# Layer 0 of a two-layer recurrent network: how the router weights reach the expert rows

## The chip, the cores and the metric

One Trainium2 chip, one of its cores. The core has five engines that run side by side: TensorE (PE), VectorE (DVE), ScalarE (ACT), GpSimd (POOL) and SyncE (SP, which here only issues DMAs), and 16 DMA engines. The metric is device time of one launch in microseconds.

## The reference, cut to what matters

The input is 16 sequences of 256 tokens, 128 channels, fp32. Two layers follow one another. Layer 0 computes `x + s * g`, where `s` is a recurrence over the tokens and `g` is the silu of a mixture of experts on the same normalised tokens:

```python
# s: for every token n, per head (8 heads, state 16 x 16)
S = exp(g)[..., None] * S + a_t[..., None] * bS[:, :, None, :] + k_t[..., None] * v_t[:, :, None, :]
# router: sigmoid scores, 4 of 8 groups, 8 of 64 experts, weights normalised, times 2.5
w_dense = jnp.zeros((T, E)).at[jnp.arange(T)[:, None], tidx].add(tw)
# experts: all 64 on all tokens, each result scaled by its router weight (0 for most)
hmid = jax.nn.silu(x @ wg) * (x @ wu)
acc + cw[:, None] * (hmid @ wdn)
```

Layer 1 (attention and a second expert block) is not touched here.

## The kernel before, in words

Layer 0 works in 8 tiles (`NT`) of 32 time steps of all 16 sequences: 512 tokens (`TOK`) a tile. In each tile two things run side by side.

- **The recurrence, on DVE.** `tile` runs 32 steps of nine instructions each (L666 to L680). Between the steps it does work for the next tile: after steps 3, 6, 7 and 12 the four stages of its layer norm (L525 to L541), after step 20 its `route` (L546 to L600), which ends with the router weights `cw`. After the last step come `finish`, `prepare_norm`, `finish_norm` and `prepare` (L612 to L651).
- **The experts, on PE, ACT and POOL.** Two experts of 64 hidden rows make a pair that fills 128 rows; there are 32 pairs and one shared expert. Before the change a pair takes three PSUM slots (`SLOTS = 3 * PAIRS + 2`), used in a ring of four: gate (three matmuls), up (three matmuls), and a third one, L486, in which a selector matrix `sel` of zeros and ones is multiplied with `cwt`, the router weights transposed. This product copies the weights of the pair's two experts to its 64 rows each, as a 128x512 tile in PSUM. ACT evicts the three slots (L380) into `act_g`, `act_u` and `act_c`, each a ring of three pairs. POOL multiplies gate by up (L302) and that by `act_c` (L306) into `hid`. PE then multiplies with the down weights, two pairs later (`LAG`, L457), into one accumulating bank.

What sets the order: each engine's program is written out, and semaphores tie them. ACT may overwrite a ring place of pair p only when `hid` of pair p - 3 is ready. In ACT's list of slots three pieces of work for the next tile are put in: `norm` at slot 24 (pair 8), `project` at pair 15, and `recurrence_inputs` at slot 66 (pair 22). After the last pair ACT copies the sum (L382), applies the silu (L384, the gate), then waits for DVE's sum of squares (L695) with L387. Only then do L357 and L362 follow; L362 copies the transposed weights `cwt` of the next tile out of PSUM, and PE starts the next tile's pairs behind it. DVE in turn waits for L387 before it can go on into its next tile. So the two sides meet once per tile at this point, and in the middle at the norm and at the projection.

SP issues every DMA: at the start inputs and weights, and in each tile the projected `z` through DRAM (L241, L244), the next tokens (L204), the gate (L248) and the result `y` (L252).

Semaphores named below: `moe_slot_filled` is PE's count of PSUM slots, `moe_slot_copied` ACT's count of evictions, `moe_hidden_ready` POOL's count of `hid`.

Of the kernel before, what the change touches and what calls it, by code (L numbers as in the profile page):

```python
# [7 lines left out]
F32 = mybir.dt.float32  # L8
F32R = mybir.dt.float32r
BF16 = mybir.dt.bfloat16  # L10
ALU = mybir.AluOpType
# [3 lines left out]
P = 128  # L15
# [3 lines left out]
TOK = B * TP  # L19
# [18 lines left out]
NEG = -1e30  # L38
SLOTS = 3 * PAIRS + 2
STEPS = 9  # L40
# [20 lines left out]
def layer0(nc, d, scratch, sem):  # L61

    z_dram, y_dram, g_dram = scratch
    with ExitStack() as ctx:
# [4 lines left out]
        ident = sb("ident", [P, P])  # L69
        onehot = sb("onehot", [P, E0])  # L70
        tri = sb("tri", [P, G0 * G0])
# [12 lines left out]
        wd = sb("wd", [P, PAIRS + 1, D])  # L84
        sel = sb("sel", [P, E0, F0], F32R)
        x_sb = sb("x_sb", [P, NS, D])
# [16 lines left out]
        cw_sum = sb("cw_sum", [P, NS])  # L103
        cws = sb("cws", [P, NS, 2 * E0], F32R)
        cwt = sb("cwt", [P, TOK], F32R)
        RING = 3
        act_g = sb("act_g", [P, RING, TOK])
        act_u = sb("act_u", [P, RING, TOK])
        act_c = sb("act_c", [P, RING, TOK])
        hid1 = sb("hid1", [P, TOK])  # L110
# [21 lines left out]
        s_eps = sem("eps_set")  # L132
        s_sel = sem("selectors_ready")
        s_w1t_ps = sem("transposed_small_in_psum")
# [21 lines left out]
        s_rt = sem("router_chain")  # L156
        s_cws = sem("router_weights_split")
        s_cwt_ps = sem("router_weightsT_in_psum")
        s_cwt = sem("router_weightsT_ready")
        s_slot = sem("moe_slot_filled")  # L160
        s_ev = sem("moe_slot_copied")
# [20 lines left out]

        LN, PREP, POST, ROUTE = 3, 20, 5, 57


        LN_AT, ROUTE_AT = (3, 6, 7, 12), 20
        PROJECT_PAIR, NORM_SLOT, INPUT_SLOT = 15, 24, 66
        SMALL = 13

# [8 lines left out]
        def _(sp):  # L198
# [8 lines left out]
            sp.dma_start(ident[:, :], d["c_ident"]).then_inc(s_small, 16)  # L207
            sp.dma_start(onehot[:, :], d["c_onehot"]).then_inc(s_small, 16)
            sp.dma_start(tri[:, :], d["c_tri"].rearrange("(o c) -> o c", o=1).to_broadcast([P, G0 * G0])).then_inc(s_small, 16)
# [69 lines left out]
        @block.gpsimd  # L279
        def _(pool):  # L280
            pool.memset(eps[:, 0:1], LN_EPS).then_inc(s_eps, 1)
            pool.memset(eps[:, 1:2], RNN_EPS).then_inc(s_eps, 1)

            for k, (w, c) in enumerate(chunks):
                pool.wait_ge(s_stage[k % 3], 16 * (k // 3 + 1) if w < 2 else 16 * (k // 3 + 2))
                parts = ([((wg_hi, wg_lo), (wu_hi, wu_lo))[w] + (c * CH * F0, CH * F0, 0)] if w < 2 else
                         [(wg_hi, wg_lo, E0 * F0, F0, 0), (wu_hi, wu_lo, E0 * F0, F0, F0)])
                for m, (hi, lo, at, n, off) in enumerate(parts):
                    src = stages[k % 3][:, off:off + n]
                    pool.tensor_scalar(hi[:, at:at + n], src, 1.0, 1.0, ALU.mult, ALU.mult).then_inc(s_hi_tmp, 1)  # L290
                    pool.wait_ge(s_hi_tmp, k + 1 + m)
                    pool.tensor_tensor(lo[:, at:at + n], src, hi[:, at:at + n].bitcast(F32), ALU.subtract).then_inc(s_split, 1)

            with pool.Fori(0, NT) as t:
                for p in range(PAIRS + 1):

                    pool.wait_ge(s_ev, t * SLOTS + min(3 * p + 3, SLOTS))
                    g, u, c = act_g[:, p % RING, :], act_u[:, p % RING, :], act_c[:, p % RING, :]
                    if p < PAIRS:
                        if p > 0:  # L300
                            pool.wait_ge(s_h, t * (PAIRS + 1) + p)
                        pool.tensor_tensor(hid1[:, :], g, u, ALU.mult).then_inc(s_h1, 1)  # L302
                        pool.wait_ge(s_h1, t * PAIRS + (p + 1))
                        if p >= 2:
                            pool.wait_ge(s_dn, t * (PAIRS + 1) + (p - 1))
                        pool.tensor_tensor(hid[:, p % 2, :], hid1[:, :], c, ALU.mult).then_inc(s_h, 1)  # L306
                    else:
                        pool.wait_ge(s_dn, t * (PAIRS + 1) + (p - 1))
                        pool.tensor_tensor(hid[0:F0, p % 2, :], g[0:F0], u[0:F0], ALU.mult).then_inc(s_h, 1)

        @block.scalar
        def _(act):
# [46 lines left out]
            def tile(t, par, ahead):  # L359

                act.wait_ge(s_cwt_ps, t + 1)
                act.activation(cwt[:, :], pb[:, 1, :], ACT.Copy).then_inc(s_cwt, 1)  # L362

                act.wait_ge(s_gst, t * 16)
                act.wait_ge(s_split, len(chunks) + 1)
                for r in range(SLOTS):
                    p, what = r // 3, r % 3
# [3 lines left out]
                    if ahead and r == 3 * PROJECT_PAIR:  # L371
                        project(t + 1, 1 - par)
                    if ahead and r == INPUT_SLOT:
                        recurrence_inputs(t + 1, 1 - par)
                    act.wait_ge(s_slot, t * SLOTS + (r + 1))
                    if what == 0 and p >= RING:

                        act.wait_ge(s_h, t * (PAIRS + 1) + (p - RING + 1))
                    dst = (act_g, act_u, act_c)[what][0:n, p % RING, :]
                    act.activation(dst, pb[0:n, r % 4, :], ACT.Silu if what == 0 else ACT.Copy).then_inc(s_ev, 1)  # L380
                act.wait_ge(s_dn, (t + 1) * (PAIRS + 1))
                act.activation(yt, pb[:, 4, :], ACT.Copy).then_inc(s_y, 1)  # L382
                act.wait_ge(s_g_ps, t + 1)
# [18 lines left out]
        def _(pe):  # L402
# [38 lines left out]
            def experts(t, par, ahead):  # L441
                pe.wait_ge(s_cws, t + 1)
                pe.wait_ge(s_ev, t * SLOTS)
# [3 lines left out]
                for s in range(NS):  # L447
                    last = pe.transpose(pb[:, 1, P * s:P * (s + 1)], cws[:, s, :].bitcast(F32), ident[:, :])
                last.then_inc(s_cwt_ps, 1)
                pe.wait_ge(s_cwt, t + 1)  # L450
                pe.wait_ge(s_sel, 1)
                pe.wait_ge(s_wd, 32)
# [13 lines left out]
                for p in range(PAIRS + 1):  # L466
                    if ahead and p == PROJECT_PAIR:
                        pe.wait_ge(s_ev, t * SLOTS + 3 * p)
                        project(t + 1, 1 - par)
                        pe.wait_ge(s_zc, (t + 2) * NS)  # L470
                        pe.wait_ge(s_sc, t + 2)
                    pe.wait_ge(s_split, 2 * (2 * p // CH + 1))
                    for what, (w_hi, w_lo) in enumerate(((wg_hi, wg_lo), (wu_hi, wu_lo))):
                        r = 3 * p + what
                        slot_free(r)
# [29 lines left out]
        def _(dve):  # L505
# [37 lines left out]
            def route(t):  # L543
# [1074 lines left out]
def constants():  # L1618
# [3 lines left out]
        "c_ident": np.eye(P, dtype=f),  # L1622
        "c_onehot": np.tile(np.eye(E0, dtype=f), (2, 1)),
        "c_tri": np.tril(np.ones((G0, G0), f), -1).reshape(-1),
# [48 lines left out]
```

## Time and profile before

| | us |
|---|---|
| median of 3 runs | 2451.81 |
| range of the runs | 2451.44 to 2452.27 |
| the profiled execution, its time | 2448.52 |
| the profiled execution, its span | 2446.7 |

The span is what the hardware profiler saw between the first and the last instruction; 1.8 us lie around it. A row of a profile is one execution. On the page, busy time is summed over instructions of an engine, and the 40 digits show in which part of the span it lies: one digit is 61.2 us. Layer 0 fills about the first 22 and a half digits and layer 1 the rest.

### The profile page before, as it was taken

The page shows a single profiled execution, that of the slowest core. Times are in us where ns is not written, and L with a number is a line of the kernel's source. Part 1 is how long each engine was busy: PE and PEld are TensorE (multiplying, and loading weights), DVE is VectorE, ACT ScalarE, POOL GpSimd, SP SyncE. Part 2 cuts the span into 40 slices and gives each one's busy share as a digit, 9 for nine tenths or more (in the row PEclk, how much of TensorE's full clock was granted, in tenths as well). Part 3 has the DMA queues.
Part 4 walks back from the last instruction along what each step waited for, and adds up shares of the span by engine and source line. Part 5 has one row for each costly group of instructions (what it writes and reads, how often), then busy time and mean ns, then how long its engine had stood idle before and what let it go on. Part 6 is the DMA issues. An engine that isn't in the chain of part 4 may idle for free. (4 is left out here: it accounts for less than half of the span.)

```text
span 2446.7 us, 35810 instructions
## 1 busy us (share of the span) xinstructions
PE 1809.3 (74%) x10242; PEld 1356.9 (55%) x10242; DVE 1758.5 (72%) x4377; ACT 1062.2 (43%) x1765; POOL 758.0 (31%) x577
## 2 busy tenths in 40 slices
PE   1585584664845855847586089898999999999998
PEld 1353352442523533425353078888888877777776
DVE  4999999999999999999999554444444434444443
ACT  2463362453634633625453045444555344444443
POOL 2764473463635644735586000000000000000000
PEclk8797797787878877977798589999999899999999
DMA  6220020200200201202000321010110100000000
GB/s 113 51 49 9 8 42 10 34 19 5 49 10 1 49 9 16 38 5 44 5 5 5 90 44 23 18 21 15 20 22 10 48 8 14 13 13 13 13 13 11
DMA packets 140823, 60.08 MB, mean 25 GB/s; under 512 B 94599, under 2 KB 135036, under 8 KB 140668
## 3 DMA queue, kind: packets, MB, share of 16 engines
q1 hardware_dynamic: 140668, 58.24, 11.8%
q8 instruction: 70, 1.15, 0.2%
q14 instruction: 85, 0.70, 0.1%
HBM read 37.10 MB, written 21.10 MB: 24 GB/s over the span
## 5 line engine op out<-in xcount | busy, mean ns | idle before, releaser
L302 POOL TENSOR_TENSOR hid<-act_g,act_u 128x512 f32<-128x512 f32 x256 | 341.1, 1332 | 530.4 <-ACT act_c L380 512.7
L405 PE MATMUL pb<-xt_hi,wg_hi 128*128 128x512 f32 (+1 forms) x264 | 211.1, 800 | 208.7 <-ACT cwt L362 168.7
L306 POOL TENSOR_TENSOR hid<-hid,act_c 128x512 f32<-128x512 f32 x256 | 344.4, 1345 | 20.1
L457 PE MATMUL pb<-hid,wd 128*128 128x512 f32 x528 | 301.9, 655 | 35.2 <-POOL hid L306 33.9
L1515 DVE SCALAR_TENSOR_TENSOR l_acc<-l_pb,l_gtok,l_acc 128x128 f32<-128x128 f32 x512 | 144.3, 344 | 253.3 <-PE l_pb L1168 253.3
L1168 PE MATMUL l_pb<-l_xt,l_big 128*128 128x512 f32 (+1 forms) x1024 | 296.3, 411 | 35.0 <-DVE l_rope L1447 25.1
L1557 DVE TENSOR_REDUCE l_mrow<-l_pb 128x2 f32<-128x256 f32 (+1 forms) x256 | 137.2, 555 | 171.4 <-PE l_pb L1168 168.4
L380 ACT ACTIVATE act_g<-pb 128x512 f32<-128x512 f32 (+1 forms) x264 | 158.3, 600 | 220.9 <-PE pb L407 215.5
L1168 PEld LDWEIGHTS l_pb<-l_big,l_hid 128*128 128x128 f32 x2048 | 247.1, 192 | 10.5
L1096 ACT ACTIVATE l_hid<-l_pb,l_cols 128x512 f32<-128x512 f32 x256 | 169.4, 688 | 183.0 <-PE l_pb L1168 182.7
L1168 PE MATMUL l_pb<-l_big,l_hid 128*128 128x128 f32 x2048 | 247.9, 275 | 0.0
L1168 PEld LDWEIGHTS l_pb<-l_xt,l_big 128*128 128x128 f32 x1024 | 192.7, 198 | 72.7 <-DVE l_rope L1447 23.7
L405 PE MATMUL pb<-xt_hi,wu_hi 128*128 128x512 f32 (+1 forms) x264 | 112.5, 426 | 154.9 <-ACT act_g L380 154.9
L405 PEld LDWEIGHTS pb<-xt_hi,wg_hi 128*128 128x128 f32 (+1 forms) x264 | 53.5, 203 | 271.9 <-ACT cwt L362 171.2
L666 DVE TENSOR_TENSOR products<-zr,rs 128x512 f32<-128x512 f32 x256 | 175.4, 685 | 14.1 <-issue 6.1
L1133 ACT ACTIVATE l_big<-l_pb 128x768 f32<-128x768 f32 x128 | 104.6, 817 | 176.0 <-PE l_pb L1327 89.5
L669 DVE TENSOR_REDUCE rs<-products 128x32 f32<-128x512 f32 x256 | 175.7, 686 | 0.0
L667 DVE TENSOR_TENSOR products<-zr,rs 128x512 f32<-128x512 f32 x256 | 174.1, 680 | 0.0
L380 ACT ACTIVATE act_u<-pb 128x512 f32<-128x512 f32 (+1 forms) x264 | 157.7, 598 | 20.0 <-PE pb L407 10.5
L457 PEld LDWEIGHTS pb<-hid,wd 128*128 128x128 f32 x528 | 89.2, 195 | 125.1 <-POOL hid L306 107.0
L380 ACT ACTIVATE act_c<-pb 128x512 f32<-128x512 f32 x256 | 152.2, 594 | 0.0
L405 PEld LDWEIGHTS pb<-xt_hi,wu_hi 128*128 128x128 f32 (+1 forms) x264 | 53.4, 202 | 174.3 <-ACT act_g L380 161.0
(300 smaller groups left out, 4105.4 us busy)
## 6 DMA issues: line engine op xcount, KB each, us to landing
z_scratch<-zs SPq DMA_DIRECT2D x128, 81.0 KB, 4.2
zr<-z_scratch SPq DMA_DIRECT2D x8, 1296.0 KB, 8.4
x_sb<-in_L_attn_x_dram SPq DMA_DIRECT2D x32, 64.0 KB, 3.1
g_scratch<-act_u SPq DMA_DIRECT2D x8, 256.0 KB, 2.3
y_scratch<-yo SPq DMA_DIRECT2D x8, 256.0 KB, 2.0
l_xs<-in_L_attn_x_dram SPq DMA_DIRECT2D x32, 64.0 KB, 1.9
l_ys<-y_scratch SPq DMA_DIRECT2D x128, 16.0 KB, 1.7
l_gs<-g_scratch SPq DMA_DIRECT2D x8, 256.0 KB, 3.0
```

The lines of the kernel that those rows point to most:

```text
L302: pool.tensor_tensor(hid1[:, :], g, u, ALU.mult).then_inc(s_h1, 1)
L306: pool.tensor_tensor(hid[:, p % 2, :], hid1[:, :], c, ALU.mult).then_inc(s_h, 1)
L380: act.activation(dst, pb[0:n, r % 4, :], ACT.Silu if what == 0 else ACT.Copy).then_inc(s_ev, 1)
L405: pe.matmul(out, l_hi, r_hi, start=first, stop=False, skip_group_check=True)
L457: last = pe.matmul(pb[:, 4, :], wd[0:n, p, :], hid[0:n, p % 2, :], start=(p == 0), stop=(p == PAIRS), skip_group_check=True)
L666: dve.tensor_tensor(products[:, 2:4], two(ZG), twice, ALU.mult).then_inc(s_st, 1)
L667: dve.tensor_tensor(products[:, 0:2], two(ZF), twice, ALU.mult).then_inc(s_st, 1)
L669: dve.tensor_reduce(rs[:, 3, 0:2], products[:, 2:4], AX.X, ALU.add).then_inc(s_st, 1)
L1096: act.activation(hid[:, r % HR, :], pb[:, 2 + r % 3, :], ACT.Relu, bias=cols[:, r:r + 1]).then_inc(s_hid, 1)
L1168: return pe.matmul(out, l, r, start=start, stop=stop, skip_group_check=True)
L1515: dve.scalar_tensor_tensor(out=acc[:, s, :], in0=pb[:, 5 + e % 2, sub], scalar=gtok[par][:, s, e:e + 1], in1=acc[:, s, :], op0=ALU.mult, o ...
L1557: dve.tensor_reduce(mrow[:, k, 2 * j:2 * j + 2], src, AX.X, ALU.max).then_inc(s_ua_dve, 1)
```

## The change

The third slot of a pair is dropped. `cwt` is kept as 64 rows of 512 tokens, one row per expert, in plain fp32. For each pair a DMA issued from ACT's own queue reads the pair's two rows, each 64 times, and writes a 128x512 tile (256 KB) into `act_c`, which is now a ring of five places (`CRING`) with a semaphore for each. The first two loads of a tile are issued right behind the copy of `cwt`, and load p + 2 stands ahead of ACT's gate eviction of pair p. POOL waits for the pair's load ahead of its second product. PE no longer multiplies by `sel`, ACT no longer evicts it, DVE no longer makes `sel` nor the split `cws`, and SP no longer loads `onehot`. The transpose of the weights becomes a product with the identity.

```diff
-SLOTS = 3 * PAIRS + 2
+SLOTS = 2 * PAIRS + 2
-        cwt = sb("cwt", [P, TOK], F32R)
-        RING = 3
+        cwt = sb("cwt", [E0, TOK])
+        RING, CRING = 3, 5
-        act_c = sb("act_c", [P, RING, TOK])
+        act_c = sb("act_c", [P, CRING, TOK])
...
-        PROJECT_PAIR, NORM_SLOT, INPUT_SLOT = 15, 24, 66
+        PROJECT_PAIR, NORM_SLOT, INPUT_SLOT = 15, 16, 44
-            sp.dma_start(onehot[:, :], d["c_onehot"]).then_inc(s_small, 16)
...
                         pool.wait_ge(s_h1, t * PAIRS + (p + 1))
+                        pool.wait_ge(*spread(t, p))
...
-                act.activation(cwt[:, :], pb[:, 1, :], ACT.Copy).then_inc(s_cwt, 1)
+                act.activation(cwt[:, :], pb[0:E0, 1, :], ACT.Copy).then_inc(s_cwt, 1)
+
+                def load_weights(p):
+                    src = cwt[2 * p:2 * p + 2, :].unsqueeze(1).to_broadcast([2, F0, TOK])
+                    act.dma_start(act_c[:, p % CRING, :], src).then_inc(s_c[p % CRING], 16)
...
+                act.wait_ge(s_cwt, t + 1)
+                load_weights(0)
+                load_weights(1)
...
+                    if what == 0 and p + 2 < PAIRS:
+                        load_weights(p + 2)
-                    dst = (act_g, act_u, act_c)[what][0:n, p % RING, :]
+                    dst = (act_g, act_u)[what][0:n, p % RING, :]
...
-                    last = pe.transpose(pb[:, 1, P * s:P * (s + 1)], cws[:, s, :].bitcast(F32), ident[:, :])
+                    last = pe.matmul(pb[0:E0, 1, P * s:P * (s + 1)], cw[:, s, :], ident[:, :], start=(s == 0), stop=True, skip_group_check=True)
...
-                    if p < PAIRS:
-                        r = 3 * p + 2
-                        slot_free(r)
-                        pe.matmul(pb[:, r % 4, :], sel[:, 2 * p:2 * p + 2, :].rearrange("p a b -> p (a b)"), cwt[:, :], start=True, stop=True).then_inc(s_slot, 1)
...
-            dve.tensor_copy(sel[:, :, :], over(onehot[:, :], F0)).then_inc(s_sel, 1)
...
-                dve.tensor_tensor(cw[:, :, :], cw[:, :, :], over(cw_sum[:, :], E0), ALU.mult).then_inc(s_rt, 1)
-                dve.wait_ge(s_rt, c.next())
-                dve.tensor_copy(cws[:, :, 0:E0], cw[:, :, :]).then_inc(s_rt, 1)
-                dve.wait_ge(s_rt, c.next())
-                dve.tensor_tensor(cws[:, :, E0:2 * E0], cw[:, :, :], cws[:, :, 0:E0].bitcast(F32), ALU.subtract).then_inc(s_cws, 1)
+                dve.tensor_tensor(cw[:, :, :], cw[:, :, :], over(cw_sum[:, :], E0), ALU.mult).then_inc(s_cw, 1)
```

The start of a tile on ACT, before the change (from the copy of `cwt` to the first eviction of pair 1):

```order
L362 ACTIVATE cwt<-pb 128x512 [waits router_weightsT_in_psum]
L364 REGISTER_ALU
L375 ISA [waits expert_weights_split,gate_stored]
L380 ACT_TABLE_LOAD
L380 ACTIVATE act_g<-pb 128x512 [waits moe_slot_filled]
L375 REGISTER_ALU
L380 ACTIVATE act_u<-pb 128x512 [waits moe_slot_filled]
L375 REGISTER_ALU
L380 ACTIVATE act_c<-pb 128x512 [waits moe_slot_filled]
L375 REGISTER_ALU
L380 ACTIVATE act_g<-pb 128x512 [waits moe_slot_filled]
```

and after it (`expert_weights_split` is the count of the expert weights that POOL splits at the start of the program; `router_weightsT_ready` tells that `cwt` is written):

```order
L364 ACTIVATE cwt<-pb 64x512 [waits router_weightsT_in_psum]
L370 REGISTER_ALU
L368 DMA act_c<-cwt 128x1x512 [waits router_weightsT_ready,expert_weights_split,gate_stored]
L368 DMA act_c<-cwt 128x1x512
L384 ISA
L368 DMA act_c<-cwt 128x1x512 [waits moe_slot_filled]
L391 ACT_TABLE_LOAD
L391 ACTIVATE act_g<-pb 128x512
L384 REGISTER_ALU
L391 ACTIVATE act_u<-pb 128x512 [waits moe_slot_filled]
L384 REGISTER_ALU
L368 DMA act_c<-cwt 128x1x512 [waits moe_slot_filled]
```

The eviction of `act_c` has gone, and a DMA issue stands ahead of every gate eviction, behind that eviction's own wait.

POOL's products of pair 2 before the change (L302 multiplies gate by up, L306 by the weights):

```order
L302 TENSOR_TENSOR hid<-act_g,act_u 128x512 [waits moe_hidden_ready]
L303 REGISTER_ALU
L306 TENSOR_TENSOR hid<-hid,act_c 128x512 [waits moe_hidden_used,moe_product_ready]
L297 REGISTER_ALU
L301 REGISTER_ALU [waits moe_slot_copied]
```

and after it:

```order
L303 TENSOR_TENSOR hid<-act_g,act_u 128x512 [waits moe_hidden_ready]
L304 REGISTER_ALU
L305 ISA [waits moe_product_ready]
L308 TENSOR_TENSOR hid<-hid,act_c 128x512 [waits moe_hidden_used,router_weights_spread2]
L298 REGISTER_ALU
```

The second product has a wait of its own on the load of its pair. It stands between the two products, and everything that POOL does later is queued behind it.

## Rows read from the trace of the kernel before

**Rows 1.** The page: busy time of each engine, and 40 slices.

```profile
PE 1809.3 (74%) x10242; PEld 1356.9 (55%) x10242; DVE 1758.5 (72%) x4377; ACT 1062.2 (43%) x1765; POOL 758.0 (31%) x577
...
DVE  4999999999999999999999554444444434444443
```

**Rows 2.** Waits of DVE from 80 to 1371 us: in total, times, longest.

```profile
DVE products L666 <- issue: 6.1, 2, 3.1
...
DVE coef L699 <- ACT coef L387: 0.4, 1, 0.4
```

**Rows 3.** Waits of ACT in the same stretch.

```profile
ACT coef L387 <- DVE coef L695: 193.4, 8, 41.7
```

**Rows 4.** The line L695: duration min/median/max in ns, first and last start.

```profile
L695 DVE TENSOR_REDUCE coef<-prod x8: 686/686/686, 224.4 to 1369.7; 128x32 f32<-128x512 f32 x8
```

**Rows 5.** Timeline of DVE at the end of route: start, duration, instruction.

```profile
1176.93 0.43 DVE L596 TENSOR_TENSOR cw<-cw,cw_sum 128x256 f32<-128x256 f32 x1
1177.39 1.27 DVE L598 CAST cws<-cw 128x256 fp32r<-128x256 f32 x1
1178.69 1.45 DVE L600 TENSOR_TENSOR cws<-cw,cws 128x256 fp32r<-128x256 f32 x1
1180.07 0.68 DVE L666 TENSOR_TENSOR products<-zr,rs 128x512 f32<-128x512 f32 x1
```

**Rows 6.** The tile cws: duration min/median/max in ns, first and last start.

```profile
L598 DVE CAST cws<-cw x8: 294/1258/1268, 45.4 to 1177.4; 128x256 fp32r<-128x256 f32 x8
L600 DVE TENSOR_TENSOR cws<-cw,cws x8: 425/1460/1470, 45.8 to 1178.7; 128x256 fp32r<-128x256 f32 x8
```

**Rows 7.** Timeline of the start: SP's issue, and DVE ahead of the projection weights.

```profile
3.08 0.43 SPq L208 DMA_DIRECT2D onehot<-in_c_onehot_dram  x1
...
11.42 2.29 DVE L512 CAST sel<-onehot 128x4096 fp32r<-128x4096 f32 x1 [10.27 <-DMA wbeta<-in_L_attn_Wbeta_dram]
15.02 0.50 DVE L515 CAST wp_hi<-products 128x648 fp32r<-128x648 f32 x1 [1.31 <-ACT products L321]
```

**Rows 8.** Removed from PE and ACT: the page's group, the line's durations.

```profile
L380 ACT ACTIVATE act_c<-pb 128x512 f32<-128x512 f32 x256 | 152.2, 594 | 0.0
...
L486 PE MATMUL pb<-cwt,sel x256: 390/397/632, 81.0 to 1316.5; 128*128 128x512 f32 x128
```

**Rows 9.** DMA from 562 to 567 us: 40 slices, queues, issues.

```profile
GB/s 0 0 0 0 0 0 0 0 0 0 16 344 393 377 360 426 181 0 0 0 0 0 0 0 0 0 0 0 0 0 0 0 131 0 0 0 0 0 0 0
...
q1 hardware_dynamic: 144, 0.26, 13.6%
...
y_scratch<-yo SPq DMA_DIRECT2D x1, 256.0 KB, 2.1
```

**Rows 10.** Timeline of the end of a tile's experts and of the next start.

```profile
695.30 1.27 POOL L306 TENSOR_TENSOR hid<-hid,act_c 128x512 f32<-128x512 f32 x1
...
700.35 0.60 ACT L384 ACTIVATE act_u<-pb 128x512 f32<-128x512 f32 x1 [0.75 <-PE pb L494]
700.96 1.28 ACT L387 ACT_TABLE_LOAD   x1
...
703.54 1.09 PE L448 MATMUL pb<-ident,cws 128*128 128x128 f32 x4 [3.23 <-issue]
```

**Rows 11.** Timeline: ACT's copy of cwt, its projection copy; DVE's stage 3.

```profile
561.64 0.58 ACT L362 ACTIVATE cwt<-pb 128x512 fp32r<-128x512 f32 x1
...
629.72 0.60 ACT L334 ACTIVATE xt_hi<-pb 128x512 fp32r<-128x512 f32 x1 [0.81 <-PE pb L424]
...
633.22 0.68 DVE L541 TENSOR_TENSOR xt_lo<-pb,xt_hi 128x512 fp32r<-128x512 f32 x1
```

**Rows 12.** Timeline: the first tile's release, and the end of layer 0.

```profile
77.89 1.28 ACT L380 ACT_TABLE_LOAD   x1 [17.49 <-POOL wu_lo L292]
...
1371.17 0.69 DVE L701 TENSOR_TENSOR yo<-yo,coef 128x512 f32<-128x512 f32 x1
```

**Rows 13.** One tile: busy us (x) of PE, PEld, DVE, ACT, POOL; PEclk, DMA share, GB/s.

```profile
561.60:725.60 164.00, 104.02 (x344) 65.38 (x344) 160.14 (x385) 73.94 (x124) 87.94 (x65) 0.82 0.12 22
```

More of the change, by code:

```diff
@@ L69, in layer0 @@
         ident = sb("ident", [P, P])
-        onehot = sb("onehot", [P, E0])
         tri = sb("tri", [P, G0 * G0])
@@ L84, in layer0 @@
         wd = sb("wd", [P, PAIRS + 1, D])
-        sel = sb("sel", [P, E0, F0], F32R)
         x_sb = sb("x_sb", [P, NS, D])
@@ L103, in layer0 @@
         cw_sum = sb("cw_sum", [P, NS])
-        cws = sb("cws", [P, NS, 2 * E0], F32R)
-        cwt = sb("cwt", [P, TOK], F32R)
-        RING = 3
+        cwt = sb("cwt", [E0, TOK])
+        RING, CRING = 3, 5
         act_g = sb("act_g", [P, RING, TOK])
         act_u = sb("act_u", [P, RING, TOK])
-        act_c = sb("act_c", [P, RING, TOK])
+        act_c = sb("act_c", [P, CRING, TOK])
         hid1 = sb("hid1", [P, TOK])
@@ L132, in layer0 @@
         s_eps = sem("eps_set")
-        s_sel = sem("selectors_ready")
         s_w1t_ps = sem("transposed_small_in_psum")
@@ L156, in layer0 @@
         s_rt = sem("router_chain")
-        s_cws = sem("router_weights_split")
+        s_cw = sem("router_weights_ready")
         s_cwt_ps = sem("router_weightsT_in_psum")
         s_cwt = sem("router_weightsT_ready")
+        s_c = [sem(f"router_weights_spread{i}") for i in range(CRING)]
         s_slot = sem("moe_slot_filled")
@@ L181, in layer0, with spread @@
         s_yst = sem("y_stored")
-        LN, PREP, POST, ROUTE = 3, 20, 5, 57
+        LN, PREP, POST, ROUTE = 3, 20, 5, 55
         LN_AT, ROUTE_AT = (3, 6, 7, 12), 20
-        PROJECT_PAIR, NORM_SLOT, INPUT_SLOT = 15, 24, 66
-        SMALL = 13
+        PROJECT_PAIR, NORM_SLOT, INPUT_SLOT = 15, 16, 44
+        SMALL = 12
+        def spread(t, p):
+            per_tile = len(range(p % CRING, PAIRS, CRING))
+            return s_c[p % CRING], (t * per_tile + p // CRING + 1) * 16
         stages = [r[:, 0:2, :].rearrange("p a b -> p (a b)") for r in (act_g, act_u, act_c)]
@@ L295, in _ @@
                 for p in range(PAIRS + 1):
-                    pool.wait_ge(s_ev, t * SLOTS + min(3 * p + 3, SLOTS))
-                    g, u, c = act_g[:, p % RING, :], act_u[:, p % RING, :], act_c[:, p % RING, :]
+                    pool.wait_ge(s_ev, t * SLOTS + 2 * p + 2)
+                    g, u, c = act_g[:, p % RING, :], act_u[:, p % RING, :], act_c[:, p % CRING, :]
                     if p < PAIRS:
@@ L361, in tile @@
                 act.wait_ge(s_cwt_ps, t + 1)
-                act.activation(cwt[:, :], pb[:, 1, :], ACT.Copy).then_inc(s_cwt, 1)
+                act.activation(cwt[:, :], pb[0:E0, 1, :], ACT.Copy).then_inc(s_cwt, 1)
+                def load_weights(p):
+                    src = cwt[2 * p:2 * p + 2, :].unsqueeze(1).to_broadcast([2, F0, TOK])
+                    act.dma_start(act_c[:, p % CRING, :], src).then_inc(s_c[p % CRING], 16)
                 act.wait_ge(s_gst, t * 16)
                 act.wait_ge(s_split, len(chunks) + 1)
+                act.wait_ge(s_cwt, t + 1)
+                load_weights(0)
+                load_weights(1)
                 for r in range(SLOTS):
-                    p, what = r // 3, r % 3
+                    p, what = r // 2, r % 2
                     n = P if p < PAIRS else F0
@@ L370, in tile @@
                         norm(t + 1)
-                    if ahead and r == 3 * PROJECT_PAIR:
+                    if ahead and r == 2 * PROJECT_PAIR:
                         project(t + 1, 1 - par)
@@ L441, in experts @@
             def experts(t, par, ahead):
-                pe.wait_ge(s_cws, t + 1)
+                pe.wait_ge(s_cw, t + 1)
                 pe.wait_ge(s_ev, t * SLOTS)
@@ L447, in experts @@
                 for s in range(NS):
-                    last = pe.transpose(pb[:, 1, P * s:P * (s + 1)], cws[:, s, :].bitcast(F32), ident[:, :])
+                    last = pe.matmul(pb[0:E0, 1, P * s:P * (s + 1)], cw[:, s, :], ident[:, :], start=(s == 0), stop=True, skip_group_check=True)
                 last.then_inc(s_cwt_ps, 1)
                 pe.wait_ge(s_cwt, t + 1)
-                pe.wait_ge(s_sel, 1)
                 pe.wait_ge(s_wd, 32)
@@ L467, in experts @@
                     if ahead and p == PROJECT_PAIR:
-                        pe.wait_ge(s_ev, t * SLOTS + 3 * p)
+                        pe.wait_ge(s_ev, t * SLOTS + 2 * p)
                         project(t + 1, 1 - par)
@@ L473, in experts @@
                     for what, (w_hi, w_lo) in enumerate(((wg_hi, wg_lo), (wu_hi, wu_lo))):
-                        r = 3 * p + what
+                        r = 2 * p + what
                         slot_free(r)
@@ L1622, in constants @@
         "c_ident": np.eye(P, dtype=f),
-        "c_onehot": np.tile(np.eye(E0, dtype=f), (2, 1)),
         "c_tri": np.tril(np.ones((G0, G0), f), -1).reshape(-1),
```

## The prediction

> **What bounds the kernel now.** I read the page first. DVE's slices are full (a 9) from the second to the 22nd, though over the span it is only 72% busy [rows 1]: layer 0 is one stretch and DVE is its engine. The waits of DVE say the same from the other side. From 80 to 1371 us its longest wait is 3.1 us, and for ACT it waits once, 0.4 us, at the very end [rows 2]. ACT waits for DVE instead, 193.4 us in 8 pieces, at the point where the two sides meet once per tile [rows 3]. So the experts have some 24 us to spare in each tile, and the length of layer 0 is DVE's: its L695 starts at 224.4 in the first tile and at 1369.7 in the last [rows 4], seven periods of 163.6 us. Layer 1 starts only after it. An edit in the expert loop is therefore worth nothing while that loop stays under DVE's period, and costs in full from there on.
>
> **What goes away.** On DVE the cast and the subtraction L598 and L600: from the end of L596 (1177.36) to the next step at 1180.07 are 2.71 us [rows 5]. The medians 1258 and 1460 ns say that it is so in nearly every tile; in the first they take 294 and 425 ns [rows 6]. The first lies in the start, so seven count: 7 x 2.71 = 19.0 us, all on DVE's path. The cast of `sel` (2.29 us) is worth nothing: behind it DVE waits 1.31 us more, for ACT's copies of the same weights [rows 7], and these depend on SP's loads, not on `sel`. One load fewer on SP ahead of the projection weights, 3.08 to the next issue at 3.56, is 0.5 us at the start. On PE 256 matmuls of 0.40 us and on ACT 256 evictions of 0.594 us go [rows 8], per tile 12.7 and 19.0 us. They lie beside DVE's work and move nothing by themselves. Removed in all: 19.5 us.
>
> **What comes in, and its price.** Each pair gets a DMA that writes 256 KB in rows of 2 KB, 128 pieces, and reads two rows of SBUF 64 times each. No DMA of the trace does that. The nearest is the store of `y`: also 256 KB in 128 pieces of 2 KB, but read from 128 rows. It is landed 2.1 us after its issue. In the 5 us around it the queue used 13.6% of 16 engines, which is 0.136 x 5.0 x 16 = 10.9 engine-us, and data flowed for seven slices of 0.13 us [rows 9]. So the fixed part is about 1.2 us, and the data part has two ends:
> - all 16 engines at once, as for `y`: 10.9 / 16 = 0.7 us a load, 32 loads in 22 us of a tile. Hidden.
> - one place through which all pieces pass in turn: 10.9 us a load at `y`'s mean rate. With the gaps between pieces filled, as in the best slice (426 GB/s, 26.6 on each of 16 engines [rows 9]), 262,144 bytes take 9.85 us.
>
> I take 9.85 us. What makes `y` fast is that each engine has rows of its own to read. Here all 128 pieces read two neighbouring rows, and a source of two rows gives nothing to spread over. That is a choice by likeness, not a measurement; both ends stay in the range.
>
> The Trainium skill has a rule for each half of this. "DMA: Bandwidth & Descriptors", section "Why a DMA increments its semaphore by 16 and not by 1": a transfer is dealt out over the largest number of engines, up to 16, that divides both access patterns' slowest dimension; here 2 and 128, so two engines. "SBUF — State Buffer", section "Door 1: The DMA port swizzle": four neighbouring partitions share one port of about 27.2 GB/s, and rows 2p and 2p + 1 always lie in one such four. An estimate from these pages is 262,144 B / 27.2 GB/s = 9.6 us a load, and by the sum below 3713 us. No row here shows either rule, since no transfer of the trace has so small an outer dimension.
>
> **The sum.** Let X be the time from one landing to the next. The first load of a tile is issued at the copy of `cwt` and lands 1.2 + X later. ACT may issue load p + 2 when `hid` of pair p - 3 is ready, so up to five are under way; while ACT does the next tile's projection the queue does not run dry if X is near 10. The last landing is then at 1.2 + 32 X. From POOL's last L306 (695.30) to the end of the gate (700.95) are 5.65 us, and to PE's transposes for the next tile (704.63) and the 0.58 us of the copy 9.9 us [rows 10, 11]. So a tile takes P = 1.2 + 32 X + 9.9. This replaces DVE's period wherever it is longer than 163.6 - 2.7 = 160.9 us, that is from X = 4.7 us on.
>
> With X = 9.85, P = 326.3 us. The first tile cannot begin before POOL has split the expert weights, at 77.9 [rows 12]. Layer 0 then ends at 77.9 + 7 x 326.3 + (1.2 + 315.2) + 5.65 + 2.6 (table load and root on ACT, two DVE instructions) = 2686.7, where it ended at 1371.86 [rows 12]. That is 1314.8 us more. The profiled execution had 2448.52 us; the median of the runs is 3.3 us above it. Sum: 2451.8 + 1314.8 = 3766.6, so **3767 us**. DVE's 19 us are in the idle time that it now has, and are not taken off.
>
> What is late next: DVE is released late twice in a tile. ACT reaches the projection at pair 15, for which `hid` of pair 12 must be ready, 1.2 + 13 X + 1.3 = 131 us after the copy of `cwt`; today DVE takes that result 71.6 us after it, and it is ready 3 us before [rows 11]. The rest it waits at the gate. Behind the waiting L308 on POOL stands every later product; PE's down matmuls wait for them, then PSUM slots and ACT's evictions. The DMA issues on ACT (0.43 us each on SP's queue [rows 7]) are shorter than the evictions that they replace, and cost nothing. SP's own DMAs take 12% of every engine in a tile, 20 us [rows 13]; if the loads are held up at the place they read from, the engines have room for that.
>
> **The rivals.**
> 1. *Two lanes side by side.* The two source rows are read by two engines that do not hinder one another: X = 10.9 / 2 = 5.44, P = 185.2, layer 0 ends at 1557.9, 186 us later, 2638 us. On two busy engines SP's 20 us a tile come on top, 8 x 20: up to 2795 us. For it: 16 engines together do read SBUF 16 times as fast as one in the row of `y`. Against it: there each has rows far from the others'. The skill's first rule without its second gives this case.
> 2. *Hidden, and faster.* The loads spread over many engines and the one source keeps up: any X under 4.7 us. Then the weights are there in time, DVE stays the bound and gets its 19.5 us: 2451.8 - 19.5 = 2432 us. This is the other side. For it: the store of `y` lands in 2.1 us, and the loads are issued two pairs ahead, at least four products of POOL or 5 us [rows 10]. Against it: the two-row source. It decides at X = 4.7; from there on each 0.1 us of X costs 8 x 3.2 = 26 us.
> 3. *One place, without filled gaps.* X = 10.88, P = 359.3, end at 2950.7: 4031 us.
>
> **How the numbers follow.** One lane (forecast, with rival 3 as its upper edge) 0.62; two lanes 0.25; hidden 0.10; something slower still, or between, 0.03. The likeliest gives 3767. The range has to reach from the two lanes at their best (2638) to the slow edge of the one lane (4031); no narrower one holds eight in ten, as the cases lie apart. Low 2630, high 4030. A measurement of this kernel tells about 0.2% (5 us) from no change. Faster by more than that is the hidden case, 0.10. No change needs X within 4.6 to 4.9 and gets 0.01. Slower is the rest, 0.89.
>
> **What the changed profile would show.** If right: in the waits POOL's L308 waits for the DMA of `act_c` in nearly all of its 256 instances, about 7 us each (9.85 less two products of POOL, 2 x 1.27 [rows 10]); issue to landing is 10 us for the first load of a tile and several times that behind others; DVE's busy time falls by about 21 us, to some 1737, and its slices to 5 or below; the copies of `cwt` lie 326 us apart; layer 1 takes the same time as before. The share of the 16 engines taken by ACT's queue tells the lanes apart from the spread: pieces of 2 KB in two engines at most. It is wrong if the copies lie under 200 us apart (two lanes) or 161 us apart (hidden), or if DVE's slices stay full. If L308 waits for ACT or PE instead, the mechanism is another.

## The result, and the profile after

| | before | after |
|---|---|---|
| median of the runs on one chip | 2452.04 us (2451.44 to 2457.21, 4 runs) | 3739.72 us (3738.4 to 3742.02, 4 runs) |
| ratio, 95% interval | | 1.5245 (1.5219 to 1.5272) |
| span of the profiled execution | 2446.7 us | 3740.2 us |
| start of layer 1 (first load, L920 after) | 1374.81 us | 2664.63 us |

The kernel became 52% slower. The forecast was 3767 us, 27 us too high. All of it is in layer 0, which is 1290 us longer. Layer 1 lasts 1071.9 us before and 1075.6 us after.

The page of after, its busy line, DVE's 40 slices and the queue of the loads (packets, MB, share of 16 engines), which answer to [rows 1]:

```profile
PE 2246.0 (60%) x10018; PEld 1488.4 (40%) x10018; DVE 1670.7 (45%) x4360; ACT 913.3 (24%) x1509; POOL 728.2 (19%) x577
...
DVE  5353438246244723724564271940144444344443
...
q10 hardware_dynamic: 33280, 67.11, 7.5%
```

DVE's row of nines has gone, and no engine is full in layer 0. The queue moves 67.11 MB, which is 256 loads of 256 KB, and keeps less than two of 16 engines busy (two would be 12.5%). Where no engine is full, the waits have to tell. All of after: in total, times, longest.

```profile
ACT act_g L391 <- issue: 1784.4, 211, 14.7
POOL hid L303 <- ACT act_u L391: 1444.1, 240, 20.3
DVE coef L700 <- ACT coef L398: 770.0, 8, 183.8
...
POOL hid L308 <- DMA act_c<-cwt: 455.9, 206, 7.7
...
DVE stat L537 <- ACT xn L329: 315.3, 8, 53.9
```

DVE, which waited 0.4 us for ACT from 80 us to the end of the layer before [rows 2], now waits 770 us at the same place: the two sides have changed roles [rows 3]. POOL waits for ACT's eviction three times as long as for the load itself, and ACT waits for "issue", which is nothing that the profile shows. The timeline of ACT in the first tile (start, duration, instruction) shows what that is:

```profile
77.40 8.38 ACTq L368 DMA_DIRECT2D act_c<-cwt  x3
85.81 1.28 ACT L391 ACT_TABLE_LOAD   x1 [25.83 <-issue]
86.05 10.26 ACTq L368 DMA_DIRECT2D act_c<-cwt  x1
...
96.35 0.60 ACT L391 ACTIVATE act_g<-pb 128x512 f32<-128x512 f32 x1 [8.17 <-issue]
96.53 10.22 ACTq L368 DMA_DIRECT2D act_c<-cwt  x1
```

Issuing three loads takes ACT 8.38 us, and each further one about 10.2 us, in which the next gate eviction stands behind it. The tile `cwt` of after (duration min/median/max in ns, first and last start) says the same of all 256 issues and gives the period:

```profile
L368 ACTq DMA_DIRECT2D act_c<-cwt x256: 522/8868/15615, 77.4 to 2621.9; - x128
L364 ACT ACTIVATE cwt<-pb x8: 573/590/590, 59.4 to 2339.5; 64x512 f32<-64x512 f32 x8
```

The eighth copy of `cwt` starts at 2339.5 us and the first load's issue at 77.4: seven tiles of 323.2 us, where a tile took 163.6 [rows 4]. The DMA view of 1060 to 1100 us, in the middle of a tile:

```profile
GB/s 25 23 25 25 25 25 25 25 25 25 23 35 25 25 25 25 33 25 25 25 25 25 23 25 25 25 25 25 25 25 25 25 35 25 25 25 25 25 25 25
...
q10 hardware_dynamic: 495, 1.00, 11.4%
```

In this stretch the flow never stops and never exceeds 35 GB/s, where the store of `y` reached 426 [rows 9]. 0.114 x 16 x 40 us is 73 engine-us for some 487 pieces of 2 KB, so 0.15 us a piece on each of two engines, and with the gaps between them a piece every 0.082 us (40 / 487). One engine of `y`'s store did nearly that alone: 2048 B at 26.6 GB/s [rows 9] are 0.077 us. At 25 GB/s a load of 262,144 B takes 10.5 us. In some stretches it is otherwise. From 1322 to 1332 us:

```profile
GB/s 33 16 33 16 33 16 25 41 49 49 49 57 49 57 49 49 49 49 49 49 49 49 41 33 25 25 25 25 25 16 33 16 33 16 33 16 33 16 33 16
```

For some 4 us both engines run at full rate, 49 to 57 GB/s. What sets them free became a question for the experiments.

The end of a tile, from POOL's last weighted product to the next copy of `cwt`, answers to [rows 10]:

```profile
1362.14 1.26 POOL L308 TENSOR_TENSOR hid<-hid,act_c 128x512 f32<-128x512 f32 x1 [4.22 <-DMA act_c<-cwt]
...
1369.38 0.60 ACT L395 ACTIVATE act_u<-pb 128x512 f32<-128x512 f32 x1 [1.21 <-PE pb L500]
...
1372.10 0.59 ACT L364 ACTIVATE cwt<-pb 64x512 f32<-64x512 f32 x1 [0.28 <-PE pb L459]
```

The last product waits for its load. From its start to the end of the copy are 10.55 us, and with the 1.2 us ahead of the first data 11.75 us of each period are fixed. So X, the time from one landing to the next, is (323.2 - 11.75) / 32 = 9.73 us. This X is a mean over two kinds of stretch: the plain ones, at 25 GB/s and 10.5 us a load, and the shorter ones in which both engines run at full rate.

### The profile page after: what moved, and what is told of

Its sections match the earlier page's. It is cut to its first block and busy times, and to the rows that moved or that the text cites. A ratio compares the mean times of both kernels' runs of the same rounds, so it can differ in the third digit from the quotient of the medians.

```text
span 3740.2 us, 35047 instructions
## 1 busy us (share of the span) xinstructions
PE 2246.0 (60%) x10018; PEld 1488.4 (40%) x10018; DVE 1670.7 (45%) x4360; ACT 913.3 (24%) x1509; POOL 728.2 (19%) x577
## 3 DMA queue, kind: packets, MB, share of 16 engines
q10 hardware_dynamic: 33280, 67.11, 7.5%
## 5 line engine op out<-in xcount | busy, mean ns | idle before, releaser
L467 PE MATMUL pb<-hid,wd 128*128 128x512 f32 x528 | 461.7, 972 | 484.0 <-POOL hid L308 484.0
L303 POOL TENSOR_TENSOR hid<-act_g,act_u 128x512 f32<-128x512 f32 x256 | 329.6, 1287 | 1445.3 <-ACT act_u L391 1444.1
L416 PEld LDWEIGHTS pb<-xt_hi,wg_hi 128*128 128x128 f32 (+1 forms) x264 | 73.0, 277 | 1068.8 <-ACT act_g L391 755.0
L308 POOL TENSOR_TENSOR hid<-hid,act_c 128x512 f32<-128x512 f32 x256 | 326.0, 1273 | 466.1 <-DMA act_c<-cwt 455.9
L467 PEld LDWEIGHTS pb<-hid,wd 128*128 128x128 f32 x528 | 118.1, 275 | 672.1 <-POOL hid L308 658.4
L1169 PEld LDWEIGHTS l_pb<-l_big,l_hid 128*128 128x128 f32 x2048 | 247.1, 192 | 10.5
L417 PE MATMUL pb<-xt_lo,wg_hi 128*128 128x512 f32 (+1 forms) x264 | 158.7, 601 | 0.0
L418 PE MATMUL pb<-xt_hi,wg_lo 128*128 128x512 f32 (+1 forms) x264 | 158.2, 599 | 0.0
L416 PE MATMUL pb<-xt_hi,wu_hi 128*128 128x512 f32 (+1 forms) x264 | 157.6, 597 | 0.0
```

The lines of the kernel that those rows point to most:

```text
L416: pe.matmul(out, l_hi, r_hi, start=first, stop=False, skip_group_check=True)
L417: pe.matmul(out, l_hi, r_lo, start=False, stop=False, skip_group_check=True)
L418: return pe.matmul(out, l_lo, r_hi, start=False, stop=True, skip_group_check=True)
L467: last = pe.matmul(pb[:, 4, :], wd[0:n, p, :], hid[0:n, p % 2, :], start=(p == 0), stop=(p == PAIRS), skip_group_check=True)
L1169: return pe.matmul(out, l, r, start=start, stop=stop, skip_group_check=True)
```

## The experiments

All times are medians; the ratio is to the kernel before, run beside on the same chip (2452 to 2457 us). P is the mean period of a tile, from the first load's issue to the last copy of `cwt`, divided by 7; X = (P - 11.75) / 32, with the fixed part of the changed kernel for all.

| kernel | median us | ratio (95%) | P | X |
|---|---|---|---|---|
| changed kernel | 3739.7 | 1.5245 (1.5219 to 1.5272) | 323.2 | 9.73 |
| e1, a DMA for each row | 3435.6 | 1.3989 (1.3964 to 1.4015) | 286.1 | 8.57 |
| e11, alternate pairs 64 rows apart | 3216.8 | 1.3117 (1.3087 to 1.3147) | 260.3 | 7.77 |
| e2, the pair's two rows 64 apart | 2710.2 | 1.1035 (1.1015 to 1.1056) | 195.3 | 5.74 |
| e9, e1 and e2 together | 2614.5 | 1.0661 (1.0636 to 1.0686) | 184.4 | 5.40 |
| e7, half the columns | 2566.3 | 1.0450 (1.0431 to 1.0469) | 178.2 | 5.20 |
| e4, no loads | 2445.9 | 0.9958 (0.9945 to 0.9972) | | |
| e3, loads from DRAM | 2408.1 | 0.9823 (0.9802 to 0.9845) | | |
| e8, e3 and the hold | 2383.4 | 0.9713 (0.9698 to 0.9728) | | |
| e5, fp32 selector, no loads | 2453.4 | 0.9997 (0.9987 to 1.0006) | | |
| e6, e5 and the hold | 2404.1 | 0.9806 (0.9793 to 0.9820) | | |
| e10, before and the hold | 2415.2 | 0.9846 (0.9831 to 0.9862) | | |

**The place or the lanes: e1 and e2.** The forecast had one place in SBUF through which all pieces pass; its rival had two engines that do not hinder one another, slow because they are only two. e1 gives each row of the pair a DMA of its own with 64 pieces as its outermost dimension, so that many engines take part but the place stays (the recorded texts call a DMA engine a lane):

```diff
-                    src = cwt[2 * p:2 * p + 2, :].unsqueeze(1).to_broadcast([2, F0, TOK])
-                    act.dma_start(act_c[:, p % CRING, :], src).then_inc(s_c[p % CRING], 16)
+                    for a in range(2):
+                        src = cwt[2 * p + a:2 * p + a + 1, :].unsqueeze(1).to_broadcast([1, F0, TOK])
+                        act.dma_start(act_c[F0 * a:F0 * (a + 1), p % CRING, :], src).then_inc(s_c[p % CRING], 16)
```

> Each pair's load is two DMAs instead of one: each reads one row of cwt 64 times and writes 64 rows, so the outermost dimension that counts is 64 and not 2. Theory A (one place: the pieces queue where the two source rows lie; the profile of the change has pieces of 2 KB at 151 ns on two lanes at once and 81 to 84 ns where only one lane or another pair's rows are read): nothing is gained, landing to landing of a pair stays near 9.7 us, a tile near 325 us, 3740 us within 60; if the pieces now run on many lanes, each takes several times 151 ns. Theory B (two lanes: only the number of engines limits): on many lanes 0.7 to 1.4 us a load, hidden, some 2430 us.

e2 keeps the single DMA, and so its engines, and parts the rows: expert 2p lies in row p and expert 2p + 1 in row 64 + p (two products of PE and two copies of ACT put them there).

```diff
-                    src = cwt[2 * p:2 * p + 2, :].unsqueeze(1).to_broadcast([2, F0, TOK])
+                    src = cwt[p:p + F0 + 1:F0, :].unsqueeze(1).to_broadcast([2, F0, TOK])
```

> cwt is laid out so that the two rows of a pair are 64 rows apart (expert 2p in row p, expert 2p + 1 in row 64 + p; two small products and two copies per tile instead of one). The load is still one DMA with an outer dimension of 2. Theory A (one place): each lane has a place of its own, pieces take 81 to 84 ns, X = 64 x 0.083 = 5.3 us, a tile 32 x 5.3 + 12.8 = 182 us, up to 202 with SP's transfers on the same two engines: 3740 - 8 x (325.7 - 182 to 202) = 2590 to 2750 us. Theory B (two lanes, slow for another reason, such as reading and writing SBUF at once): pieces stay at 151 ns and the time at 3740 us.

The DMA view of e1, 1000 to 1010 us, and then of e2, 700 to 710 us:

```profile
GB/s 25 8 25 25 49 25 8 25 33 41 25 8 25 33 41 33 0 25 33 41 25 16 33 25 57 57 107 98 107 41 49 66 33 49 33 57 0 16 33 41
...
q10 hardware_dynamic: 228, 0.37, 81.3%
```

```profile
GB/s 49 49 49 49 49 49 49 49 49 49 49 49 49 49 49 49 49 49 49 49 49 49 49 49 49 49 49 49 49 49 49 49 49 49 49 49 57 41 33 33
...
q10 hardware_dynamic: 236, 0.48, 12.9%
```

e2 moved the rows alone, and the rate went from 25 to 49 GB/s on the same two engines (12.9% of 16), X from 9.73 to 5.74 us, the time to 2710 us as expected. e1 kept some thirteen engines busy at a time (81.3% of 16) and mostly got what two had got, at some 0.73 us a piece instead of 0.15. This window has 37 GB/s because a fast stretch lies in it; by its X of 8.57 us e1 has 31 GB/s, where the changed kernel's 9.73 us are 27. So the place is the limit, and engines are not. Rival 1 of the forecast is refuted: with two free engines the changed kernel would have been e2, which lies inside that rival's 2638 to 2795 us. But the theory of one place missed e1 by 304 us, and e1 has slices of 107 GB/s like the stretch of 49 to 57 above. A second form of it (A2 in the recorded texts) fits both: several loads are under way, an engine that runs ahead reads rows of the next pairs, and if those lie in another place, the two no longer meet.

**The second form, the bytes, and both cures: e11, e7, e9.** e11 leaves a pair's rows adjacent and puts every second pair 64 rows away:

```diff
-                    src = cwt[2 * p:2 * p + 2, :].unsqueeze(1).to_broadcast([2, F0, TOK])
+                    src = cwt[F0 * (p % 2) + 2 * (p // 2):F0 * (p % 2) + 2 * (p // 2) + 2, :].unsqueeze(1).to_broadcast([2, F0, TOK])
```

> One DMA a pair with an outer dimension of 2 as in the change, the pair's rows side by side; but pair p's rows lie in the lower half of cwt for even p and 64 rows further for odd p (the router weights then go to other experts). Theory A2: as long as both lanes work on the same pair they share a place and take 151 ns a piece; when one is a pair ahead, both run at 84 ns, and nothing brings them together again: X between 5.6 and 9.7, 2700 to 3740 us, with pieces of both lengths. Theory A as first told, without the lanes drifting: 3740 us.

e7 loads 256 of the 512 columns, in as many pieces:

```diff
+                    src = cwt[2 * p:2 * p + 2, 0:TOK // 2].unsqueeze(1).to_broadcast([2, F0, TOK // 2])
+                    act.dma_start(act_c[:, p % CRING, 0:TOK // 2], src).then_inc(s_c[p % CRING], 16)
```

> The loads carry 256 of 512 columns, in pieces of 1 KB (the other half of the tile is a constant 1, so half of the tokens are weighted with 1). Theory A and the sum (time goes with the bytes through one place, a tile is 32 X + 12.8): X = 4.9 us, a tile 170 us, 3740 - 8 x (325.7 - 170) = 2494 us. If a piece has a fixed cost of some size c beside its bytes, X is 4.9 + 64 c, and each 10 ns of c are 8 x 32 x 0.64 = 164 us more. If the limit were ACT's blocked issue, with the number of pieces as its price: 3740 us.

e9 has the rows of e2 and a DMA for each row as in e1.

> Both edits at once: the pair's rows lie 64 rows apart, and each is read by a DMA of its own with an outer dimension of 64. The DMA of one row per expert gained 300 us although I expected nothing. Theory A2 (a place serves some 27 to 31 GB/s however many lanes ask; a gain comes only when lanes run ahead into another row's DMA and so keep two places busy): with neighbouring DMAs always at two places, X falls to 5 to 7 us, 2560 to 2800 us, and pieces take from under 0.6 to 1.1 us. Theory E (many lanes make one place itself faster): X stays near 8.3 as with the rows together, 3400 us.

In e11 no load alone has two places to read from, only neighbouring loads together, and 523 us came back, within the wide range of the second form and far from the 3740 us of the first. That engines which work on different loads release one another, when these lie 64 rows apart, is thus shown. That the fast stretches of the changed kernel come about in the same way, between pairs whose rows are close together, is argued from it; no view shows which row an engine reads. How large a place is, no run here tells beyond that rows 2p and 2p + 1 share one and rows 64 apart do not. In e7 X fell from 9.73 to 5.20: to 53% for half the bytes in the same number of pieces. The time is that of bytes. By the two means some 0.7 us a load does not shrink, but in its plain stretches e7 has 23 to 25 GB/s (640 to 680 us), so part of that can be fewer fast ones. e7 took 2566 us where 2494 were expected without such a part, and e9 came inside the range of the second form. e9 shows how little engines add once there are two places. Its DMA view, 700 to 710 us:

```profile
GB/s 57 41 33 49 49 49 57 66 49 74 41 98 16 49 57 66 66 57 66 49 49 41 57 49 66 66 33 66 57 66 25 74 49 49 74 33 33 123 57 33
...
q10 hardware_dynamic: 329, 0.54, 86.2%
```

Fourteen engines give 54 GB/s where two gave 48: two places at about 27 each, the rate of one of `y`'s engines [rows 9].

**Another source: e3.** `cwt` is stored to DRAM once a tile, and both rows of a pair are read from there, 64 times each:

```diff
+                        src = c_dram[par, 2 * p + a:2 * p + a + 1, :].to_broadcast([F0, TOK])
+                        act.dma_start(act_c[F0 * a:F0 * (a + 1), p % CRING, :], src).then_inc(s_c[p % CRING], 16)
...
+                act.dma_start(c_dram[par], cwt[:, :]).then_inc(s_cst, 16)
+                act.wait_ge(s_cst, (t + 1) * 16)
```

> The changed kernel, but cwt is first stored to DRAM (128 KB a tile), and each pair is loaded from there in two DMAs of 64 rows each. Theory A (the one place in SBUF was the limit) : with a source outside SBUF and an outer dimension of 64 a load takes about 1 us of 16 engines, all hidden, POOL waits for next to nothing; time as without loads, 2440 to 2450 us, and ACT's issues fall from 8.9 us to under 1 us. Rival: 64 reads of one row of 2 KB meet in one place in DRAM too: issue times and waits stay, 2600 us or more.

2408 us, 1.8% faster than before. e3 and e1 have the same two DMAs of 64 rows a pair and differ in the source alone (and in the store): 2408 against 3436 us. The same bytes go to the same rows of `act_c`, so neither the destination nor the volume was the limit. The text had expected 2440 to 2450 us; where the other 32 us and more come from is told with e8. The issues of e3:

```profile
L370 ACTq DMA_DIRECT2D act_c<-c_scratch x512: 452/617/1417, 79.5 to 1271.7; - x171
```

Twice as many issues at 0.6 us each: the 8.9 us of the changed kernel are not the price of an issue. They go at the pace of the transfers (10.2 us where a load takes 10.5), which fits a wait for room in a queue that drains slowly.

**The removal alone: e4.** The changed kernel without `load_weights` and POOL's wait for it.

```diff
-                        pool.wait_ge(*spread(t, p))
...
-                load_weights(0)
-                load_weights(1)
...
-                    if what == 0 and p + 2 < PAIRS:
-                        load_weights(p + 2)
```

> The changed kernel without its 256 loads and the wait on them: POOL multiplies by what lies in act_c (the experts are weighted with wrong numbers). It shows what the removals alone are worth. The sum of the prediction: DVE loses cast and subtraction, 19.0 us, and the start 0.5 us: 2452 - 19.5 = 2432.5 us. Rival: DVE's two-operand instructions wait for POOL's at other places now (DVE's busy time in the changed kernel fell by 88 us, not by 22), so that up to 8 us a tile more or less may come: 2380 to 2450 us.

The end of DVE's work came 7.4 us earlier (its last sum of squares starts at 1362.3, before at 1369.7 [rows 4]); beside the runs of before the median is 0.42% lower, some 10 us. The forecast had 19.5. The groups of DVE (busy us, mean ns) in e4 from 80 to 1372 us, then the same two instructions before, from 80 to 1371 us:

```profile
L561 DVE TENSOR_TENSOR cmp_eq<-cmp_eq,tri 128x256 f32<-128x256 f32 x7 | 9.7, 1387 | 0.2
...
L563 DVE TENSOR_TENSOR cmp_gt<-cmp_gt,cmp_eq 128x256 f32<-128x256 f32 x7 | 9.6, 1369 | 0.2
```

```profile
L564 DVE TENSOR_TENSOR cmp_eq<-cmp_eq,tri 128x256 f32<-128x256 f32 x7 | 3.0, 426 | 0.2
...
L566 DVE TENSOR_TENSOR cmp_gt<-cmp_gt,cmp_eq 128x256 f32<-128x256 f32 x7 | 3.0, 425 | 0.2
```

The two removed instructions took 8.8 + 10.2 us in these seven tiles, at 1258 and 1460 ns; in the first tile, where POOL is idle, 294 and 425 [rows 6]. About 1 us of each was the meeting with POOL's products. Take them away, and DVE and POOL meet at two other instructions, which grow from 0.43 to 1.38 us: 13.3 us come back there, while `xn` and `biased` lose some 5, and some smaller ones take these 5 back (`penalty<-penalty`, for one, grows from 394 to 684 ns). That leaves 6 of the 19 us.

**Where the meeting costs most: e5, e6, e10, e8.** e5 keeps the selector product, but in fp32 on 64 rows, so that DVE's cast and subtraction go and nothing is loaded:

```diff
-        sel = sb("sel", [P, E0, F0], F32R)
+        sel = sb("sel", [E0, E0, F0])
...
-                dve.tensor_copy(cws[:, :, 0:E0], cw[:, :, :]).then_inc(s_rt, 1)
-                dve.wait_ge(s_rt, c.next())
-                dve.tensor_tensor(cws[:, :, E0:2 * E0], cw[:, :, :], cws[:, :, 0:E0].bitcast(F32), ALU.subtract).then_inc(s_cws, 1)
```

> The kernel before with one part of the change alone: no cast and subtraction of the router weights on DVE; the selector product stays and is done in fp32 on 64 rows of cwt. PE: a product of about 1.0 us a pair instead of 0.40, some 20 us a tile, beside DVE's work, which leaves 24. Theory C (removals alone are worth what the run without loads showed, since freed DVE time comes back as waits of other two-operand instructions for POOL): 2440 to 2447 us. Theory D (the prediction's term, 19 us): 2433 us. Rival: PE's extra 0.6 us a pair makes the experts late: slower than 2452.

No change (0.9997), so neither theory's time came. DVE's busy time fell by 28.9 us to 1729.6, but its waits from 80 to 1372 us have a new line:

```profile
DVE xt_lo L540 <- ACT xt_hi L333: 25.4, 7, 4.1
```

PE's slower products put the experts behind DVE, and what DVE saved it waits for. The hold is one wait of POOL ahead of the first product of a tile. It lets DVE finish its preparation of the recurrence first:

```diff
                 for p in range(PAIRS + 1):
+                    if p == 0:
+                        pool.wait_ge(s_pr, (t + 1) * PREP)
```

e6 is e5 with it, e10 the kernel before with it and nothing else, e8 is e3 with it.

> As the run before, and POOL's first product of a tile also waits until DVE has finished prepare of that tile. Theory C: DVE's six two-operand instructions at the end of prepare (1.65 to 1.77 us each before, 0.69 in the slow kernel, where POOL is mostly idle) no longer meet POOL, 6 x 1.0 us x 7 tiles = 42 us off DVE's path, 2395 to 2415 us. Against it: POOL starts some 9 us later in each tile, which uses up part of the 24 us that the experts have to spare, and moves other meetings; if the norm or the projection becomes late, 2440 us or more.

> The kernel before, with one wait more: POOL's first product of a tile waits for the end of prepare on DVE. Theory C: DVE's six instructions at the end of prepare take 0.69 us again, 42 us less, 2405 to 2415 us. If what DVE gains there is met again in layer norm and route: 2430 to 2450 us.

> As the run from DRAM, and POOL's first product of a tile waits for the end of prepare. Theory C: 42 us less than the run from DRAM, 2395 to 2410 us. If it is slower than its fellow with the selector product, the loads cost something that DVE or POOL sees.

The group of DVE for L643 before, from 80 to 1371 us, and the same instruction in e10, from 80 to 1372 us:

```profile
L643 DVE TENSOR_TENSOR zr<-zr,coef 128x512 f32<-128x512 f32 x7 | 11.6, 1654 | 0.2
```

```profile
L645 DVE TENSOR_TENSOR zr<-zr,coef 128x512 f32<-128x512 f32 x7 | 4.8, 692 | 0.2
```

It is one of six alike (1651 to 1765 ns before). Six times 7 tiles times 1 us are some 42 us, and e10's layer 0 ended 37.5 us earlier (tile `coef` of e10; before 1369.7 [rows 4]):

```profile
L697 DVE TENSOR_REDUCE coef<-prod x8: 685/686/686, 224.4 to 1332.2; 128x32 f32<-128x512 f32 x8
```

So one added wait is worth 37 us by itself, 49 on top of e5, and 25 on top of e3. e6 came inside its range, e10 at the edge of its own, and e8 below the 2395 to 2410 us expected. e3 is less improved because its trip through DRAM already holds POOL back. POOL's first product of a tile, before and then in e3, in tiles whose copy of `cwt` starts at 561.64 [rows 11] and at 542.04 us:

```profile
566.40 1.84 POOL L302 TENSOR_TENSOR hid<-act_g,act_u 128x512 f32<-128x512 f32 x1 [32.85 <-ACT act_c L380]
```

```profile
551.79 1.28 POOL L304 TENSOR_TENSOR hid<-act_g,act_u 128x512 f32<-128x512 f32 x1 [34.65 <-ACT act_u L395]
```

It starts 4.8 us after the copy before and 9.8 us after it in e3, and there the first of the six instructions is undisturbed and the last is not (80 to 1372 us):

```profile
L648 DVE TENSOR_TENSOR zr<-zr,coef 128x512 f32<-128x512 f32 x7 | 4.8, 692 | 0.2
...
L656 DVE TENSOR_TENSOR zr<-zr,prod 128x512 f32<-128x512 f32 x7 | 11.7, 1678 | 0.2
```

The six together take 71 us before, 50 in e3 and 29 in e8. So e3 has a part of the hold built in. Its layer 0 ends 39 us earlier than that of e4, which has no loads at all (last sum of squares at 1323.5 and 1362.3 us): 21 us are these six, and 13 are `cmp_eq` and `cmp_gt`, which stay at 0.43 us in e3. e8, 2383.4 us, is faster than both kernels, by 2.9% than before. What lets `zr<-zr,coef` and the others suffer where some instructions beside them do not was not tried.

## Why the prediction was right, and where not

- **The bound.** Right. DVE's period of 163.6 us gave way to that of the experts, and the edit cost in full from there.
- **The price of a load.** Right in mechanism: one place, taken by likeness to one engine of `y`'s store and tried by e2 and e9. In size it was near by some luck: 9.85 us forecast, 9.73 measured, but only as a mean. In plain stretches a load takes 10.5 us. Had it stayed so, 8 x 32 x 0.77 us, nearly 200 us, would come on top and the kernel take near 3940 us, an estimate, still inside the range but some 170 us above the forecast. The fast stretches, which the forecast did not have, brought the mean back to it. The Trainium skill ("SBUF — State Buffer", "Door 1: The DMA port swizzle") gives a port 27.2 GB/s, by which a load is estimated at 9.6 us. The plain stretches at 25 GB/s lie 8% below that rate, and two places at 54 GB/s in e9 agree with it; its groups of four partitions no run here shows. The rule of the Trainium skill on how many engines a transfer is dealt to ("DMA: Bandwidth & Descriptors", "Why a DMA increments its semaphore by 16 and not by 1") agrees: 11.4% of 16 with an outermost dimension of 2, 81 and 86% with 64.
- **The sum.** P 323.2 against 326.3, from X 3.8 us too high over 32 loads and a fixed part 0.65 us too low (11.75, not 11.1). Layer 0 grew by 1290.3 us instead of 1314.8: seven periods account for 22 of the 24.5 us.
- **"The DMA issues on ACT ... cost nothing."** Wrong. They were priced at SP's 0.43 us [rows 7], whose queue drains. Here a median of 8.87 us passes in each, with ACT standing behind it. By the 25 GB/s, some 0.7 of a load had moved when the third issue ended, so a little over two loads fit ahead, an estimate, where the forecast had up to five under way. The total did not change, since the transfers still follow each other without a gap inside a tile; what changed is who waits. POOL's L308 waits 2.2 us for its load (455.9 / 206), not 7, and L303 waits 1444 us for ACT. The text had said that a wait for ACT would mean another mechanism. That test was badly chosen: a full queue shows as a wait for the engine that issues, and only e2 and e3 could tell the two apart.
- **What is late next.** Half right. DVE waits at the projection, 291 us in seven tiles, and at the gate, 770 us. A third place was missed: `xn` of layer norm's stage 1 (L537, 315 us). ACT's norm comes at eviction 16, pair 8, and these evictions now follow the loads. The projection copy came 150.4 us after the copy of `cwt` (1047.41 to 1197.82), not 131. Some 8 of these 19 us are its 13 loads at 10.5 instead of 9.85 us. The rest fits the issues ahead of it, which hold up ACT as well: that of load 16 ended only at 1195.4, 148 us after the copy.
- **The removals.** Mis-sized, which the forecast time did not feel: 10 us, not 19.5. Rival 2 was priced at 2432 us by them; e4, where the loads cost nothing at all, took 2446. e3, in which the loads are hidden, took 2408, since it also moves POOL's start, a term that the forecast did not have.
- **DVE's busy time** fell by 88 us, not 21. In the waits at the gate POOL is idle, and the preparation behind it runs undisturbed: `zr<-zr,coef` takes 692 ns after, as in e10. It went unseen since DVE waits anyway.

## What to carry to other kernels

Before a DMA replaces an on-chip broadcast, ask from how many separate rows it reads, and not only how many bytes or engines it has: re-reading one or two SBUF rows for 256 KB costs 8.6 to 9.7 us, and the same two rows read from DRAM were hidden. A DMA issue is cheap only while its queue drains; on a compute engine a full queue stops the work behind it, and the profile shows that as a wait for the engine, or for nothing. When an instruction on the bound takes three to four times its own time in some places, its removal gives back only what its neighbours do not then lose; moving the other engine's work away from that stretch gave more than the removal.

## What the hardware showed unexpectedly

- An issue on ACT's queue lasted up to 15.6 us (median 8.87) when the loads behind it were slow, and 0.62 us in e3 when they were fast.
- More engines on one source row make each piece slower, and the sum hardly faster: 0.15 us a piece on two engines and 0.73 on thirteen, while the mean rate over the loads went from 27 to 31 GB/s (9.73 and 8.57 us for 262,144 B); the second form of the theory puts that difference down to rows of different places read at once.
- Two engines that read the same place share 25 GB/s for long, but for some microseconds they run at 49 to 57 GB/s (1322 to 1332 us of after). That they then work on different loads is the reading that e11 supports.
- DVE and POOL slow each other at some instructions: DVE's by about 1 us (692 to 1654 ns), POOL's products from 1.27 to 1.6 us and more (1.84 us at 566.40 of before). A hold of POOL at the start of each tile, which avoids the meeting there, made the whole kernel 1.5% faster.
